# Layer 1 of a four-layer graph network: the 49 products of a counted bundle in one run instead of seven runs between counted tiles

## The reference, cut to what matters

```
edge_index = jnp.stack([src, dst])
h = jnp.maximum(_layernorm(x, axis=-1), 0.0)
x = x + _L0_gnn_ref(h, edge_index, L0_gnn_W, L0_gnn_b)
...
src, dst = (edge_index[0], edge_index[1])
neighbor_sum = jax.ops.segment_sum(x[src], dst, num_segments=x.shape[0])
neighbor_count = jax.ops.segment_sum(jnp.ones((src.shape[0],), dtype=x.dtype), dst, num_segments=x.shape[0])
neighbor_mean = neighbor_sum / jnp.clip(neighbor_count, 1.0)[:, None]
h = jnp.concatenate([x, neighbor_mean], axis=-1)
return h @ W.T + b
```

## Time and profile before

| | |
|---|---|
| median of 3 runs | 6154.61 us (6154.51 to 6168.87) |
| profiled execution | 6172.62 us |
| its span | 6170.1 us |
| granted TensorE clock, mean over the span | 0.816 |
| TensorE matmul busy | 4210.8 us, 68% |
| VectorE busy | 2962.1 us, 48% |
| layer 1's counted part | from about 160 to 1061 us of the span |

### The profile page before, as it was taken

The page is one execution under the profiler, slowest core; times in us unless marked ns, Lnnn a source line. Parts: engine busy times, 40 slices in busy tenths (PEclk is TensorE's granted clock), DMA queues, the critical chain, the costliest instruction groups (busy, mean ns, idle before and its releaser), DMA issues.

```text
span 6170.1 us, 75714 instructions
## 1 busy us (share of the span) xinstructions
PE 4210.8 (68%) x23505; PEld 3296.0 (53%) x23515; DVE 2962.1 (48%) x10025; ACT 1552.4 (25%) x5818; POOL 3670.6 (59%) x3828
## 2 busy tenths in 40 slices
PE   4889999565555555555555488877688888888432
PEld 3455665554545445554555366643466676666432
DVE  7777676554445555555555533343343333332222
ACT  5333333322223233333332301122011111111000
POOL 4344443566666666666666356646566666665665
PEclk7799999776677777777677699988799999999666
DMA  3233343544444444444444355555111111111121
GB/s 109 94 115 131 133 146 122 153 136 136 136 136 136 134 140 137 146 138 137 137 147 136 128 181 197 192 176 186 48 45 45 44 43 45 44 45 41 43 62 46
DMA packets 307373, 701.31 MB, mean 114 GB/s; under 512 B 71121, under 2 KB 153901, under 8 KB 294685
## 3 DMA queue, kind: packets, MB, share of 16 engines
q0 software_dynamic: 156112, 371.60, 21.8%
q1 hardware_dynamic: 148844, 323.93, 15.2%
q10 hardware_dynamic: 2016, 0.92, 0.1%
HBM read 565.11 MB, written 131.05 MB: 113 GB/s over the span
## 4 chain that ended last, share of the span: by engine, by line
PE 37%; another core or an unknown queue 24%; DVE 20%; issue 13%; ACT 4%; DVEq 1%; SPq 1%; DMA 0%; ACTq 0%
PE ps L2621 11%; DVE oneh L1900 6%; PE ps L2516 5%; PE ps L2528 5%; PE ps L2577 4%; DVE ps L2035 3%; PE ps L2606 3%; DVE third L2027 2%; PE ps L2584 2%; PE ps L2644 2%; PE ps L2465 1%; DVE tmp L1991 1%; ACT h L1669 1%; PE ps L2537 1%
## 5 line engine op out<-in xcount | busy, mean ns | idle before, releaser
L1507 POOL DMA_INDIRECT rows<-tab_rel,third x1203 | 1186.7, 986 | 645.5 <-issue 333.1
L1507 POOL DMA_INDIRECT rows<-tab_hp,idx_src x1120 | 1089.3, 973 | 577.1 <-issue 305.4
L1507 POOL DMA_INDIRECT rows<-tab_h,idx_src x810 | 787.2, 972 | 810.9 <-PE ps L2584 465.2
L2644 PE MATMUL ps<-third 128*128 128x128 f32 x3126 | 622.7, 361 | 669.2 <-issue 374.0
L2644 PEld LDWEIGHTS ps<-third 128*128 128x128 f32 x3126 | 556.5, 266 | 729.1 <-issue 412.7
L2621 PE MATMUL ps<-third,h 128*120 128x385 bf16 (+20 forms) x4606 | 879.6, 338 | 72.7 <-issue 29.7
L1718 ACT ACTIVATE turned_words<-turned_words 128x128 f32<-128x128 f32 x1563 | 464.5, 300 | 1145.5 <-DVE turned_words L2040 830.5
L2621 PEld LDWEIGHTS ps<-third,h 128*120 128x120 bf16 (+10 forms) x4606 | 592.0, 132 | 290.6 <-issue 55.5
L2577 PE MATMUL ps<-oneh,rows 128*128 128x128 f32 x2406 | 385.9, 312 | 290.5 <-DVE oneh L1900 177.2
L1507 POOL DMA_INDIRECT third<-tab_hp,idx_src x443 | 430.8, 972 | 217.1 <-issue 121.5
L2577 PEld LDWEIGHTS ps<-oneh,rows 128*128 128x128 f32 x2406 | 347.1, 221 | 337.9 <-DVE oneh L1900 199.1
(11 more groups left out here) (285 smaller groups left out, 5858.2 us busy)
## 6 DMA issues: line engine op xcount, KB each, us to landing
third<-dst_flat SPq DMA_DIRECT2D x390, 256.0 KB
h<-cnt_d SPq DMA_DIRECT2D x48, 1568.0 KB
cnt_d<-h SPq DMA_DIRECT2D x46, 1568.0 KB
tab_rel<-third SPq DMA_DIRECT2D x49, 512.0 KB
rows<-tab_rel,third POOLq DMA_INDIRECT x1203
rows<-tab_hp,idx_src POOLq DMA_INDIRECT x1120
rows<-tab_h,idx_src POOLq DMA_INDIRECT x810
third<-tab_hp,idx_src POOLq DMA_INDIRECT x443
```

The lines of the kernel that those rows point to most:

```text
L1507: pool.indirect_dma_start(out=to[:, t, 0:n], out_offset=None, in_=table[:, :], in_offset=bass.IndirectOffsetOnAxis(ap=idx[:, col:col + 1], ...
L2644: last = pe.matmul(ps_t[sl][:, t * P:(t + 1) * P], onehT[:, sl, t * P:(t + 1) * P], pwin[:, st["v"] % 2, :], start=True, stop=True)
```

## The change

In layer 1 the generator gives all 49 products at its first step, at the price of seven steps, and none at the six behind it. The layers that do not count keep steps of seven. `pack_out`, `pack_turn` and `pack_add` keep their distances in steps. A wait for the end of all `split_lo` is added ahead of `keys3_rows`.

```diff
@@ multiply(u)
-                for q0 in range(0, nb, MULTIPLY_STEP):
-                    plan.append(("pack_mm", dict(st, q0=q0, q1=min(nb, q0 + MULTIPLY_STEP))))
-                    yield MULTIPLY_STEP * H3 / 2.4
+                step = nb if layer == 0 else MULTIPLY_STEP
+                for q0 in range(0, nb, step):
+                    plan.append(("pack_mm", dict(st, q0=q0, q1=min(nb, q0 + step))))
+                    yield step * H3 / 2.4
@@ plan_edges
                 if layer == 2 and turn in KEYS3_TURNS:
+                    keys3["lo"] = s_lo.value
                     plan.append((KEYS3_TURNS[turn], keys3))
@@ vector_program
                 elif kind == "keys3_rows":
+                    dve.wait_ge(s_lo.handle, st["lo"])
                     vector_keys3_rows(dve)
```

## The result

The changed kernel takes 6348.98 us (median of 4 runs, 6336.47 to 6355.34) against 6159.6 us of the kernel before (4 runs). The ratio is 1.0303, 95% interval 1.0282 to 1.0325: slower by 3%, or 189 us. The forecast had the sign and the place, and a third of the size: 6213 us, range up to 6255.

A forecast was written before the change was run, and what follows sets the result against it. PE was taken to bound layer 1's products and DVE's pairs the counts behind them; 47.8 us of pairs plus 10 us of clock gave 58 us on 6154.6, so 6213 us, range 6165 to 6255.

The forecast's parts named there:

- PE's own work is the same: Layer 1's products: still 49, 8.05 us a run; interleaving counts costs PE nothing, so joining the runs saves nothing by itself.
- Six pairs of head start lost, 48 us: Layer 1's counts behind the products: DVE must make six more pairs there for each bundle, 47.8 us in all.
- the first term: Pairs' loss for bundles 0 to 12 (w 3 to 9): 13 x 1.4 = 18.2 us, called if anything low.
- One or two scatters, `pack_out` later, at no net cost: Directly behind layer 1's run: scatters follow and delay `pack_out`, replacing the same 0.9 us that left the phase of products.
- The clock: 8 more slow starts, 10 us: Layer 1's products after longer idle phases: some 8 more bundles start at half clock, 1.2 us each, 10 us.
- Rival C: Layer 1's products: the unbroken run holds full clock and slow starts vanish; 6114 us, or 6139 from starts alone; chance 0.07.
- Gathers stay ahead: Layer 1's gathers behind the run: rows are fetched five groups ahead, so no cost was put on them.
- The range: Whole kernel: 6165 us, pairs partly hidden, to 6255, with all starts slow and 10 us for waits that fall together.

The follow-up runs named there:

- e15: The changed kernel as it stands, on a 5400 chip: 5453.51 us against 5404.71 for the kernel before.
- e8: The kernel before with five pair buffers instead of seven, on a 6155 chip: 6194.18 us against 6161.85.
- e10: The kernel before with five products between counted tiles instead of seven for bundles of 10 packs and more, on a 6155 chip: 6138.09 us against 6161.85.
- e5: The kernel before with layer 1's gathered rows replaced by SyncE's loads of consecutive rows, on a 5400 chip: 5398.51 us against 5397.65.
- e6: The changed kernel with layer 1's gathers replaced by SyncE's loads, on a 5400 chip: 5442.83 us against 5397.65 for the kernel before.
- e1: The changed kernel with the run's price paid over seven steps, on a 5400 chip: 5463.28 us against 5397.65 for the kernel before.
- e14: The changed kernel with the run's price paid over seven steps, again on a 5400 chip: 5458.71 us against 5404.71 for the kernel before.
- e19: The changed kernel with the run's price paid over seven steps, again on a 5400 chip: 5467.24 us against 5392.49 for the kernel before.
- e21: The changed kernel with the run's price paid over seven steps, on a 6155 chip: 6367.9 us against 6172.62 for the kernel before.
- e20: The changed kernel with layer 1's gathers replaced by SyncE's loads, on a 6155 chip: 6200.27 us against 6172.62 for the kernel before.
- e7: The changed kernel as it stands, on a 6155 chip: 6341.33 us against 6161.85 for the kernel before, ratio 1.0285.
- e2: The kernel before with a bundle's whole price paid at its first seven products, on a 5400 chip: 5410.24 us against 5397.65.
- e12: The kernel before with layer 1's gathers replaced by SyncE's loads, again on a 5400 chip: 5387.34 us against 5404.71.
- e18: The kernel before with layer 1's gathers replaced by SyncE's loads, again on a 5400 chip: 5397.83 us against a median of 5392.49.
- e13: The changed kernel with layer 1's gathers replaced by SyncE's loads, again on a 5400 chip: 5445.92 us against 5404.71 for the kernel before.

## Why the prediction was right or wrong

- **PE's own work is the same.** Right. At full clock it is 8.05 us from the run's first product to the next instruction, 49 times what a product took before; its row shows 8.2 us on both kinds of chip.
- **Six pairs of head start lost, 48 us.** Right in mechanism, and in size where nothing else interferes: 49 us in e15, and 45 us in the counted part with the rows by SyncE. e8 and e10 move the head start by -2 and +3 pairs and give +21 to +32 and -24 us. That the sum fits so well is in part luck. By the starts of the bundles' products in e5 and e6, bundles 0 to 12 lost 11 us (18.2 in the sum), 13 to 24 lost 19 (15.6), 25 to 44 lost 17 (14.0), and the last one gained 1; the remark that the first term was if anything low was wrong.
- **One or two scatters, `pack_out` later, at no net cost.** Right as to where: DVE resumes 3.7 us after the run at w = 10. Spreading the turns (e1, e14, e19, e21) gained nothing; it cost 5 us more than the change on the one chip that ran both (5458.71 against 5453.51), which is within what single executions tell.
- **The clock: 8 more slow starts, 10 us.** Wrong in number on either chip. With 8.3 us for a run that starts at full clock and 8.8 or more for one that does not, I count 10 of 44 slow ones in e15 and 26 of 44 in the changed kernel on the 6155 chip, against 13 before; without gathers it is 5 with the one run and 7 with the order before (e6, e5), where I had expected 8 more. The granted clock there is 0.87 from 685 to 1061 us, 0.99 before. It is not a cause by itself: over 200 to 1000 us it is 0.88 in the changed kernel and 0.95 in e20, on such a chip, with the same run and no gathers. The low clock follows the idle time between the late signals. It carries a part of the loss: the 46 runs take 426 us in all in the changed kernel and 396 in e15, so 29 of the 140 us by which the two counted parts differ lie in the products and 111 in the phases of counts. Rival C had the wrong sign. So had, for this kernel, the advice of the Trainium skill ("TensorE: Matmul & The Clock Gate", section "HAM oscillation — how this bites in real kernels") to run all tiles of a contraction before the engine waits for data; the page's case has such waits between the tiles. Here there was hardly a gap within the products to close, since counts filled it; the gaps lay behind them and grew.
- **"Gathers stay ahead": the step that failed.** I counted gathers only as to whether rows are in time, and they are. What I left out, and so put at nothing, is that GpSimd's gathers, 8 or 9 a bundle, go along with late signals between the engines on these chips, and that the change moves them. By the timelines of the kernel before, 241 of the 395 gathers behind the first products are issued while products run, where PE has work stored and VectorE slack, and 154 in the phases of counts; after the change it is 35 and 360. In these phases each count, pair and copy waits for another engine's signal, and the signals come late. On a 5400 chip the gathers move in the same way (51 and 344 in e15), and the change costs no more with them than without (49 and 45 us). The missing term is 180 - 49 = 131 us on a 6155 chip (e7, e15). The counted parts give the same account: 881 us without gathers and 902 with them before, 926 and 1086 after, so 45 us of the 183 are there without gathers and 138 come only with them. The trace of before had the sign of it: ScalarE waits 59.5 us on issue in the layer, which no trace of that order from a 5400 chip shows (e2, e12, e18), and in layer 2 VectorE waits for something the profile calls remote for a third of the time. I read neither.
- **The range.** Its upper end took in all slow starts and 10 us for waits that fall together. It had no term for engines that wait longer beside GpSimd, since none of my rivals was about GpSimd at all.

What stays open: why signals come late during and behind rows of gathers on some chips and not on others, and why hardly while a tile's counts take one bank. e20 takes away several things at once: the gathers' instructions, their many scattered rows, and the queue that they use. None was tried alone.

## What to carry to other kernels

Where an engine has a phase in which it is far ahead and one in which it is chased, work that feeds the second phase belongs between the pieces of the first; joining the pieces saves nothing if their interleaving was free, and shorter pieces were better still here. When an edit moves one engine's work in time, list what every other queue now does in the phase that has become critical, GpSimd's gathers among it, not only whether it is in time. Time a change on more than one chip before its size is believed: here the same edit cost 49 us and 180.

## What the runs showed of the hardware that I had not expected

- Chips, or their states, differ: the same kernel before takes 5387 to 5405 us on three and 6155 to 6175 on others. It is not the speed of the engines: without gathers in layer 1, the clock of the one run's three stretches is 0.86, 0.99 and 1.00 on either kind (e13, e20) and its counted part as long within 2 us, and in a row of gathers an instruction of 0.95 us starts every 1.25 us on both (e15, after).
- On the 6155 chips, signals between PE, VectorE and ScalarE came 1 to 3 us late in phases with eight gathers in a row (ScalarE's wait of 2.47 us ahead of 1147.03), and phases of counts with two banks a tile took 13.4 to 16.9 us, where they took 9.2 to 11.5 in the same program on a 5400 chip (e15). With no gathers by GpSimd they took 9.0 to 11.3 there as well (e20).
